# A decoder layer's last projection merged into the routing phase, and the experts' second weights loaded one phase later

## What is computed

```python
out = jnp.einsum('bhqk,bhkd->bqhd', attn, v).reshape(B, Sd, E)
x = x + out @ W_o + b_o                          # second output projection
xf = _layernorm(x, axis=-1).reshape(BN, D)       # BN = 4096 tokens
gate_scores = xf @ gate_W + gate_b               # (4096, 4)
topk_scores, topk_idx = jax.lax.top_k(gate_scores, 2)
weights = jax.nn.softmax(topk_scores, axis=-1)
# expert e: h = relu(LN(xf @ W1[e] + b1) * g1 + be1);  y = LN(h @ W2[e] + b2) * g2 + be2
x = x + (sum of the two weighted y + xf)
```

## Time and profile before

| | us |
|---|---|
| median of 3 runs | 4606.11 (4603.25 to 4610.75) |
| the profiled execution | 4606.11 |
| its span, first to last instruction | 4604.4 |
| "out2": first DMA issue to the start of the next phase | 3610.3 to 3724.8 |
| `route`: to the start of the next phase | 3724.8 to 4066.3 |
| `experts`: until DVE passes the wait for the last lists | 4066.3 to 4122.5 |
| `experts`: the rest | 4122.5 to 4604.4 |

### The profile page before, as it was taken

One profiled execution on the slowest core, in us unless ns is written; L12 is line 12 of the kernel. 1 busy time (PEld: TensorE's weight loads), 2 busy tenths in 40 slices (PEclk: granted clock), 3 DMA queues, 4 the chain that ended last, 5 costly groups with the idle time before them and its releaser, 6 DMA issues. The chain is left out here.

```text
span 4604.4 us, 61752 instructions
## 1 busy us (share of the span) xinstructions
PE 4057.2 (88%) x21906; PEld 2506.8 (54%) x21906; DVE 2742.5 (60%) x4978; ACT 2095.8 (46%) x3869; POOL 2478.5 (54%) x927
## 2 busy tenths in 40 slices
PE   6998999997779998999999999999999653439997
PEld 5874555555568885444444444444444432328886
DVE  4436777772443336777777777777775332216665
ACT  2113555553121111666666666666666222216665
POOL 0001333331000002999999999999999224528887
PEclk9997999998889997999999999999999865569998
DMA  4546344314555555222222222222220465524444
GB/s 147 173 164 144 87 105 110 87 40 148 186 187 172 172 169 135 54 56 58 56 56 56 56 56 56 56 56 56 56 56 6 162 182 100 84 61 74 82 80 64
DMA packets 283654, 449.72 MB, mean 98 GB/s; under 512 B 31960, under 2 KB 132312, under 8 KB 277208
## 3 DMA queue, kind: packets, MB, share of 16 engines
q1 hardware_dynamic: 259640, 407.27, 33.9%
q0 software_dynamic: 19776, 36.85, 4.7%
q10 hardware_dynamic: 3968, 2.10, 0.2%
HBM read 267.22 MB, written 178.91 MB: 97 GB/s over the span
## 5 line engine op out<-in xcount | busy, mean ns | idle before, releaser
L665 POOL TENSOR_TENSOR cross_partial<-cross_partial,cross_probs 128x2048 f32<-128x2048 f32 x320 | 1465.7, 4580 | 66.5 <-ACT cross_probs L832 29.4
L881 DVE TENSOR_REDUCE cross_neg_max<-cross_scores 128x1 f32<-128x512 f32 x2048 | 1265.7, 677 | 395.2 <-PE cross_scores L708 395.1
L832 ACT ACTIVATE cross_probs<-cross_shifted 128x512 f32<-128x512 f32 x2048 | 1074.5, 606 | 743.3 <-PE cross_shifted L720 709.2
L708 PE MATMUL cross_scores<-cross_k_stack,cross_q_stack 96*128 96x512 f32 x2048 | 875.9, 437 | 39.4 <-DVE cross_neg_max L881 27.4
L720 PE MATMUL cross_shifted<-cross_q_stack,cross_k_stack 98*128 98x512 f32 x2048 | 850.6, 420 | 13.8 <-DMA cross_q_stack<-cross_neg_dram 5.8
L720 PEld LDWEIGHTS cross_shifted<-cross_q_stack,cross_k_stack 98*128 98x128 f32 x2048 | 387.2, 190 | 385.4 <-issue 236.4
L708 PEld LDWEIGHTS cross_scores<-cross_k_stack,cross_q_stack 96*128 96x128 f32 x2048 | 395.0, 193 | 287.2 <-DVE cross_neg_max L881 224.6
L832 ACT ACTIVATE self_probs<-self_shifted 128x512 f32<-128x512 f32 (+3 forms) x768 | 358.6, 492 | 367.1 <-PE self_shifted L723 286.2
L881 DVE TENSOR_REDUCE self_neg_max<-self_scores 128x1 f32<-128x512 f32 (+3 forms) x768 | 388.4, 548 | 208.1 <-PE self_scores L708 108.2
L736 PE MATMUL cross_out<-cross_probs,cross_v 128*32 128x512 f32 x4096 | 494.1, 600 | 0.0
L708 PE MATMUL self_scores<-self_k_stack,self_q_stack 96*128 96x512 f32 (+3 forms) x768 | 308.2, 422 | 23.6 <-DMA self_k_stack<-k_hi 10.0
(11 more groups left out here) (249 smaller groups left out, 6294.6 us busy)
## 6 DMA issues: line engine op xcount, KB each, us to landing
cross_k_stack<-k_hi SPq DMA_DIRECT2D x30, 1024.0 KB, 20.1
out_a_in<-attn SPq DMA_DIRECT2D x16, 1024.0 KB, 9.7
x<-out_y SPq DMA_DIRECT2D x16, 1024.0 KB, 5.3
kv_x_in<-in_ctx SPq DMA_DIRECT2D x16, 1024.0 KB, 5.4
k_hi<-kv_out_hi SPq DMA_DIRECT2D x64, 256.0 KB, 2.6
k_lo<-kv_out_lo SPq DMA_DIRECT2D x64, 256.0 KB, 3.2
v<-kv_out_n SPq DMA_DIRECT2D x64, 256.0 KB, 2.3
cross_v<-v SPq DMA_DIRECT2D x32, 512.0 KB, 25.1
```

Of the source, the lines that this page charges most:

```text
L665: nc.gpsimd.tensor_tensor(total, total, own, ALU.add).then_inc(pool_added.sem, 1)
L708: mm = nc.tensor.matmul(scores[at][:, 0:width], q_st[0:96, w, h, q0:q0 + P], k_st[0:96, w, h, half * WIDE:half * WIDE + width], start=True ...
L832: nc.scalar.activation(probs[:, e % NE % PB, h, f:], shifted[n % SHIFTED][:, f:], ACT.Exp).then_inc(exped.sem, 1)
L881: nc.vector.tensor_reduce(neg_max[:, q % 2, column(a), half:half + 1], scores[n % (SLOTS * ROUNDS) % AHEAD][:, 0:width], AX.X, ALU.max, ne ...
```

## The change

`project_out` is no longer called for the second projection, and `x2` is gone. `route` becomes `finish`, which also projects: for chunk c+2 PE makes 14 matmuls a tile (12 and 2 that add the bias: a matrix of which only the first row is one, times a matrix of which only the first row is the bias, high and low part). They stand between the gate scores of chunk c and their turning. DVE adds the residual, which lies in `x_in`, now with 3 buffers; the sum stays there and is what statistics and normalising read. The attention output has one split buffer (`a_hi`, `a_lo`), so ACT's split of a chunk waits for the projection of the chunk before. A row load of chunk c+3 now waits for the store of chunk c, which has just been issued. Only the 4 first matrices of the experts are loaded and split here, one in two iterations. The 4 second ones are loaded by SP and split by ACT and DVE at the beginning of `experts`, in buffers that are not yet in use for other things; the rows `g2` and `be2`, and behind them the list loads of 31 steps, wait until two and three of them are split.

```diff
-def route(nc, name, src, gate_w, gate_b, w1, w2, xn, out, lists, w_hi, w_lo, table, valid, ident, neg_half):
+def finish(nc, name, attn_t, out_w, out_b, residual, gate_w, gate_b, w1, xn, out, lists, w_hi, w_lo, table, valid, ident, neg_half):
...
-        x_in = sb("x_in", [P, 2, TPC, D])
+        x_in = sb("x_in", [P, 3, TPC, D])
+        a_in = sb("a_in", [P, 2, KT, CH])
+        a_hi = sb("a_hi", [P, KT, CH], F32R)
+        a_lo = sb("a_lo", [P, KT, CH], F32R)
+        ow_hi = sb("ow_hi", [P, KT, D], F32R)
+        ow_lo = sb("ow_lo", [P, KT, D], F32R)
+        first_row = sb("first_row", [P, P], F32R)
+        bias = sb("bias", [1, D])
+        bias_hi = sb("bias_hi", [P, D], F32R)
+        bias_lo = sb("bias_lo", [P, D], F32R)
...
+            def load_attention(c):
+                after(sp, a_lo_ready, c - 1)
+                sp.dma_start(a_in[:, c % 2], attn_v[c // 2, :, :, c % 2 * CH:(c % 2 + 1) * CH]).then_inc(a_loaded[c % 2], 16)
             def load(c):
-                after(sp, base_stored[c % 2], 16 * (c // 2))
-                sp.dma_start(x_in[:, c % 2], tiles_of(src)[c]).then_inc(loaded[c % 2], 16)
+                after(sp, base_stored[c % 3], 16 * (c // 3))
+                sp.dma_start(x_in[:, c % 3], tiles_of(residual)[c]).then_inc(loaded[c % 3], 16)
             def load_weight(m):
+                if m == 1:
+                    sp.wait_ge(ow_lo_ready, 1)
                 after(sp, w_lo_ready, m - 1)
-                sp.dma_start(raw[:, m % 2], (w1, w2)[m % 2][m // 2].rearrange("(k p) n -> p k n", p=P)).then_inc(raw_loaded[m % 2], 16)
+                sp.dma_start(raw[:, (m + 1) % 2], w1[m].rearrange("(k p) n -> p k n", p=P)).then_inc(raw_loaded[(m + 1) % 2], 16)
+            sp.dma_start(raw[:, 0], out_w.rearrange("(k p) n -> p k n", p=P)).then_inc(raw_loaded[0], 16)
+            load_attention(0)
             load(0)
+            sp.dma_start(bias[:, :], out_b.rearrange("(o d) -> o d", o=1)).then_inc(small, 16)
             sp.dma_start(gw[:, :, :], gate_w.rearrange("(k p) e -> p k e", p=P)).then_inc(small, 16)
             sp.dma_start(gb[:, :], gate_b.rearrange("(e o) -> e o", o=1)).then_inc(small, 16)
+            load_attention(1)
             load(1)
+            load_attention(2)
+            load(2)
             load_weight(0)
-            load_weight(1)
             for c in range(CHUNKS):
+                if c + 3 < CHUNKS:
+                    load_attention(c + 3)
                 sp.wait_ge(normed, TPC * (c + 1))
                 sp.dma_start(tiles_of(xn)[c], x_n[:, c % 2]).then_inc(xn_stored[c % 2], 16)
                 sp.wait_ge(based, TPC * (c + 1))
-                sp.dma_start(tiles_of(out)[c], x_in[:, c % 2]).then_inc(base_stored[c % 2], 16)
-                if c >= 1 and c + 1 < CHUNKS:
-                    load(c + 1)
-                if c >= 1 and c + 1 < 2 * EXPERTS:
-                    load_weight(c + 1)
+                sp.dma_start(tiles_of(out)[c], x_in[:, c % 3]).then_inc(base_stored[c % 3], 16)
+                if c + 3 < CHUNKS:
+                    load(c + 3)
+                if c % 2 == 0 and c // 2 + 1 < EXPERTS:
+                    load_weight(c // 2 + 1)
...
+            def attention_high(c):
+                act.wait_ge(a_loaded[c % 2], 16 * (c // 2 + 1))
+                after(act, acc_ready, TPC * c)
+                nc.scalar.activation(a_hi[:, :, :], a_in[:, c % 2], ACT.Copy).then_inc(a_hi_ready, 1)
...
+            act.wait_ge(raw_loaded[0], 16)
+            nc.scalar.activation(ow_hi[:, :, :], raw[:, 0], ACT.Copy).then_inc(ow_hi_ready, 1)
+            attention_high(0)
+            act.wait_ge(small, 48)
+            act.wait_ge(made, 15)
+            nc.scalar.activation(bias_hi[0:1, :], bias[:, :], ACT.Copy).then_inc(gw_hi_ready, 1)
             nc.scalar.activation(gw_hi[:, :, :], gw[:, :, :], ACT.Copy).then_inc(gw_hi_ready, 1)
+            attention_high(1)
             normalise(0)
             for c in range(CHUNKS):
+                if c + 2 < CHUNKS:
+                    attention_high(c + 2)
...
-                weight_high(c)
+                if c % 2 == 0:
+                    weight_high(c // 2)
...
+            def attention_low(c):
+                dve.wait_ge(a_hi_ready, c + 1)
+                nc.vector.tensor_tensor(a_lo[:, :, :], a_in[:, c % 2], a_hi[:, :, :].bitcast(F32), ALU.subtract).then_inc(a_lo_ready, 1)
+            def add_projection(c):
+                dve.wait_ge(loaded[c % 3], 16 * (c // 3 + 1))
+                for t in range(TPC):
+                    dve.wait_ge(acc_ready, TPC * c + t + 1)
+                    nc.vector.tensor_tensor(x_in[:, c % 3, t], acc[t % 2][:, :], x_in[:, c % 3, t], ALU.add).then_inc(added, 1)
...
+            dve.wait_ge(ow_hi_ready, 1)
+            nc.vector.tensor_tensor(ow_lo[:, :, :], raw[:, 0], ow_hi[:, :, :].bitcast(F32), ALU.subtract).then_inc(ow_lo_ready, 1)
+            attention_low(0)
+            dve.wait_ge(gw_hi_ready, 2)
+            nc.vector.tensor_tensor(bias_lo[0:1, :], bias[:, :], bias_hi[0:1, :].bitcast(F32), ALU.subtract).then_inc(gw_lo_ready, 1)
             nc.vector.tensor_tensor(gw_lo[:, :, :], gw[:, :, :], gw_hi[:, :, :].bitcast(F32), ALU.subtract).then_inc(gw_lo_ready, 1)
-            dve.wait_ge(made, 11)
+            dve.wait_ge(made, 15)
+            add_projection(0)
+            attention_low(1)
             variance(0)
             scales(0)
+            add_projection(1)
             for c in range(CHUNKS):
+                if c + 2 < CHUNKS:
+                    attention_low(c + 2)
...
-                    weight_low(c - 1)
+                if c % 2:
+                    weight_low(c // 2)
+                if c + 2 < CHUNKS:
+                    add_projection(c + 2)
                 gate(c)
...
+            def project_tokens(c):
+                pe.wait_ge(a_lo_ready, c + 1)
+                for t in range(TPC):
+                    after(pe, added, TPC * c + t - 1)
+                    i = 0
+                    for part, w in ((a_hi, ow_hi), (a_hi, ow_lo), (a_lo, ow_hi)):
+                        for k in range(KT):
+                            nc.tensor.matmul(acc[t % 2][:, :], part[:, k, t * P:(t + 1) * P], w[:, k, :], start=i == 0, stop=False)
+                            i += 1
+                    nc.tensor.matmul(acc[t % 2][:, :], first_row[:, :], bias_hi[:, :], start=False, stop=False)
+                    nc.tensor.matmul(acc[t % 2][:, :], first_row[:, :], bias_lo[:, :], start=False, stop=True).then_inc(acc_ready, 1)
+            pe.wait_ge(ow_lo_ready, 1)
+            pe.wait_ge(gw_lo_ready, 2)
+            pe.wait_ge(made, 15)
+            project_tokens(0)
+            project_tokens(1)
...
                 mm.then_inc(scored, 1)
+                if c + 2 < CHUNKS:
+                    project_tokens(c + 2)
                 pe.wait_ge(rows, c + 1)
...
+        in_t2 = t2[:, :, :, :].rearrange("p u t d -> p (u t) d")
+        staged = [in_t2, rows[:, :, 2], rows[:, :, 3], in_t2]
...
+            def load_second(e):
+                sp.dma_start(staged[e], w2[e].rearrange("(k p) n -> p k n", p=P)).then_inc(w2_in[e], 16)
             for s in range(STEPS):
                 at = sp.value_load(table[0:1, s, 1:2], min_val=0, max_val=EXPERTS * BATCH * SEQ - TOK)
                 sp.dma_start(entries[:, s], lists[bass.ds(at, TOK), :].rearrange("(p t) w -> p t w", t=TT)).then_inc(lists_in[s >= FIRST_LISTS], 16)
                 if s == FIRST_LISTS - 1:
-                    for n, vec in enumerate((b1, b2, g2, be2)):
-                        for e in range(EXPERTS):
-                            sp.dma_start(rows[:, e, n, :], vec[e:e + 1, :].to_broadcast([P, D])).then_inc(rows_in[n], 16)
-                        if n == 0:
-                            for k, col in enumerate((g1, be1)):
-                                sp.dma_start(cols[:, k], col.rearrange("e (k p) -> p e k", p=P),
-                                             allow_slow_non_contiguous=True).then_inc(cols_in, 16)
+                    load_rows(0)
+                    for e in range(3):
+                        load_second(e)
+                    load_rows(1)
+                    for k, col in enumerate((g1, be1)):
+                        sp.dma_start(cols[:, k], col.rearrange("e (k p) -> p e k", p=P),
+                                     allow_slow_non_contiguous=True).then_inc(cols_in, 16)
+                    sp.wait_ge(w2_lo_ready, 1)
+                    load_second(3)
+                    sp.wait_ge(w2_lo_ready, 2)
+                    load_rows(2)
+                    sp.wait_ge(w2_lo_ready, 3)
+                    load_rows(3)
...
+                if s == 0:
+                    pe.wait_ge(w2_lo_ready, EXPERTS)
                 pe.wait_ge(ht_lo_ready, s + 1)
...
+                if s == -3:
+                    for e in range(EXPERTS):
+                        second_high(e)
+                    act.wait_ge(cols_in, 32)
...
+            def second_low(e):
```

(46 more changed lines are left out.)

42 lines of the change are left out of this document (24 added, 18 removed).

## The result

The changed kernel takes 4499.51 us (median of 4 runs, 4497.08 to 4499.94), the one before 4608.43 (4603.25 to 4612.87) in the same comparison: ratio 0.9765 (95% interval 0.9753 to 0.9777). The prediction was 4512.0, with a range of 4476 to 4562. The profiled execution has a span of 4498.2 against 4604.4: 106.2 us less, where 93.8 were forecast.

The account below looks back on a forecast made before the run. The old path was taken as a projection bound by PE, then a routing on one load at a time. The merged phase gains 103.3 us, the experts' opening gives back 9.5: 4606.1 - 93.8 = 4512.3 us, range 4476 to 4562.

Parts of the forecast that it names:

- PE starts: Opening of the merged phase: PE's first projection starts at 3626, with bounds of 3623 and 3630.
- from there to iteration 0: Opening: two projections of 14.6 us each, with 4.4 us of splits and signalling between, so iteration 0 starts at 3659.6.
- iteration 0: First iteration of the merged loop: 30.9 us, being 36.7 less 5.8 for counting no earlier tokens.
- iterations 1 to 5: Merged loop: 36.7 us each on PE's chain, from 20.8 + 2.6 + 12.9 + 0.4.
- iteration 6 to `experts`: Loop's end without projections: from 3874.0, through list writes and a kept POOL stall of 5.94 us, to 3963.0.
- experts' opening: Start of `experts` until DVE is past the last lists: 65.7 us, 9.5 more than before (bounds +4 and +15).
- rest: The part of `experts` behind its opening: the 482 us there stay unchanged.
- warm: Rival: PE keeps 2.4 GHz over counting and gate scores, up to 5 us less in 6 iterations, 4482; chance 0.12.
- the DMA cover is thin: Merged loop: 4.5 MB a chunk at 128 GB/s take 36.8 us, equal to PE's chain; taken as just hidden.
- DMA: Rival: SP's queue, not PE, sets the iteration at 44 us, 7.3 more in each of 6, 4556; chance 0.20.
- the circle on SP: Old routing: SP stands 219.8 us at the weight load for a low part DVE makes only after the next rows.
- fetching the longer program: A few us added to "DMA" for the range's upper end, 4562.

Follow-up runs that it names:

- e4: The change with 1 MB more stored by SP's queue in every chunk, to a tensor nobody reads; 4492.62 us, ratio 0.9794 to the kernel before.
- e9: The change with DVE adding the bias, two of four projected tiles inside the turning, attention splits double-buffered and a chunk earlier, single raw weight buffer; 4452.67 us.
- e8: The change with biases, gains and second weights at the experts' opening issued by ACT's queue instead of SP's; 4480.58 us, ratio 0.9757 to the kernel before.
- e1: The kernel before with only the second weights moved into `experts`; projection unmerged, two row buffers, rows one chunk ahead; 4538.09 us, ratio 0.9889.
- e2: As e1, but three row buffers and rows loaded three chunks ahead, projection still unmerged; 4506.50 us, ratio 0.9822 to the kernel before.
- e3: The change with two row buffers instead of three, rows asked for two chunks ahead; 4495.12 us, ratio 0.9799 to the kernel before.
- e5: The change as it is, run again beside other experiments on another chip; 4494.82 us, ratio 0.9788 to the kernel before.
- e7: The change with the bias added to the residual rows by DVE, 12 matmuls a tile instead of 14; 4482.27 us, ratio 0.9761 to the kernel before.
- e11: e9 with experts' biases, gains, second weights on ACT's queue, but small-element loads on SP among lists and POOL's gains wait later; 4439.07 us.

## Why the prediction was right, and where it was off

The direction, the mechanism and nearly every stage held. Against the profile after:

| step | predicted | measured | difference |
|---|---|---|---|
| PE starts | 3626 | 3623.62 | -2.4 |
| from there to iteration 0 | 33.6 | 34.45 | +0.9 |
| iteration 0 | 30.9 | 30.0 | -0.9 |
| iterations 1 to 5 | 5 x 36.7 = 183.5 | 172.1 | -11.4 |
| iteration 6 to `experts` | 89.0 | 89.4 | +0.4 |
| experts' opening | 65.7 | 67.1 | +1.4 |
| rest | 481.9 | 481.5 | -0.4 |

The result lies well inside the range. The sum of the differences is -12.4, which is the span of 4498.2 against the 4510.6 that belongs to 4512.3.

**The mis-sized term** is the iteration, and in it the last part. Turning and counting were forecast at 8.5 + 2.6 + 5.8 and measured 10.96 + 5.83: right. Gate scores, projection and turning back were forecast at 6.4 + 12.9 + 0.4 = 19.7 and measured 17.6. The old 6.4 us had three parts, as the trace of before shows: the score matmuls to the end of the last (5.28), PE's wait for ACT's copy of the scores (0.77), and the turning back (0.34). In the new order the wait and the last 0.2 us of the matmuls' run-out lie under the projection: 1.0 us. I had carried that time over as if the projection stood behind it. Another 0.4 is the gate that DVE begins behind the last addition: it does (3757.73, at the addition's end), but PE does not lose by it, as the turning with its waits took no longer than forecast. The remaining 0.7 is the clock: it rises while the gate scores are still running, as windows of the profile after show:

```profile
3768.00:3774.00 6.00, 6.00 (x31) 6.00 (x29) 0.84 (x3) 4.50 (x7) 0.00 (x0) 0.50 0.50 118
...
3776.00:3777.00 1.00, 1.00 (x4) 0.25 (x2) 0.69 (x1) 0.00 (x0) 1.00 (x1) 0.50 0.79 293
3777.00:3778.00 1.00, 1.00 (x4) 0.33 (x3) 0.00 (x0) 0.00 (x0) 0.69 (x2) 0.64 1.00 383
3778.00:3779.00 1.00, 1.00 (x6) 0.65 (x4) 0.00 (x0) 0.25 (x1) 0.87 (x1) 1.00 1.02 377
```

A granted clock of 0.50 is 1.2 GHz and 1.00 is 2.4. That the projection would find full speed was right. The rival "warm" had part of the truth only: the turning begins at 2.4 GHz, but in its first wait the clock falls (0.83 in the us from 3760, 0.50 from 3762), and the counting runs at 1.2 GHz.

**PE's start.** I took 3626 between 3623 and 3630; it was 3623.62, so the small loads did not delay it.

**The judgement that was wrong, though it changed no term**, is that the DMA cover is thin. I took 128 GB/s from a turn of the old loop as a rate that the queue can reach. It was the length of one old turn, the slowest of five, not a limit. e4 moved 168 GB/s at no cost, so 0.20 for "DMA" was too much. The mechanism of that rival, SP late behind the landing of a store, is real: it takes 12.0 us of SP at most in the change, where it costs nothing, and 28.1 in e9, where it does. With the thin cover goes the reading that I set beside it: the Trainium skill's advice (Perfetto Trace Analysis, DMA Optimizations) of separate issuing engines for inputs and outputs would hardly have brought anything in this loop, where no engine waits for a load and SP waits for x_n for 130.6 us; that is argued, no run splits the loop's queue. In e9's shorter loop it might. At the experts' opening a second issuing engine, though not split by inputs and outputs, was worth 15.5 us of that stage (e8).

**Where the gain came from.** The prediction opened with the circle on SP and went on to credit the merge. That was its weak side: it summed the whole phase and never asked what each part would give alone. On one chip the parts read: breaking the circle 50.7 us, after the 10 us or so that the longer opening takes back (e1), loading rows further ahead 31.6 more (e2), merging 11.4 (e3). On the chip of e5 the change saves 96.8 us instead of 109, as the kernel before is 17 us faster there and the changed one 5. Why the old kernel differs more from chip to chip was not tried; that its loop waits for transfers is a guess at the reason.

**What would have shown me wrong**, and did not: ACT or DVE waiting for `a_in` (never in the loop, 0.74 us at the opening) or `x_in` (never), over 25 us a chunk at `base_stored` (longest 12.0), 0.43 us a matmul in the projection (0.23), over 15 us lost in `experts` (10.5). The upper end of the range held a few us for fetching the longer program. No run shows such a term.

## What to carry to other kernels

Look for a wait inside a queue that issues several kinds of transfers: whatever stands behind it is late too, and if the waited-for work needs what stands behind it, the loop runs at the latency of the circle. Moving that one load by an iteration was worth two thirds of a rewrite. When work is moved into a loop's idle engine, take the chain's parts between their ends, not a stretch with its waits, and put the moved work where the engine waits: with half of each chunk's tiles inside the turning, and their splits made a chunk ahead, the phase was 27.4 us shorter than with all of them behind it (e9, e7; the two steps were not tried apart). And when a loop has become shorter, read the issuing queue's own waits again: in e9 one of them makes one iteration twice as long as the others.

## What the runs showed that was not expected

- Two transfers of 8 KB, made of 4-byte elements, are issued one behind the other. The issue of the second took 9.00 us on SP behind 5 MB of loads (the change), 10.41 us on ACT's queue (e8), and 4.76 us on SP among list loads (e11).
- List writes can leave more to the bulk transfers than the 91 GB/s of the earlier trace rows had me think. A window of e4 that lies wholly under list writes (one each 1.27 us) has 241 GB/s:

```profile
3778.00:3786.00 8.00, 7.17 (x38) 5.67 (x36) 2.87 (x12) 0.66 (x2) 6.17 (x7) 1.00 1.15 241
```

- The stall of POOL inside the last list writes is in every kernel of the study that I read for it: 5.94, 6.50 and 5.53 us (before, the change, e9), each time between the first and the second write of chunk 7. Its cause was not looked for.
